# Scores in slot 19 instead of 23 of a two-layer graph kernel's schedule, with the steps that depend on x at other places in the engines' slots

## The reference, cut to what matters

```python
# layer 0
mask = (adj > 0); deg = sum(mask, axis=1)
agg  = mask @ x / max(deg, 1)
out0 = relu(concat(x @ W_self + b_self, agg @ W_nb + b_nb) @ W_comb + b_comb)
x    = layernorm(x + out0)
# layer 1
neib_att = tanh(neigh @ Wn1 + bn1) @ Wn2 + bn2        # 4096 x 32
value    = neigh @ Wv + bv                            # 4096 x 128
x_att    = tanh(x @ Wx1 + bx1) @ Wx2 + bx2
ws       = leaky_relu(x_att @ neib_att.T, 0.01)
ws       = softmax(where(adj > 0, ws, -9e15), axis=1)
out1     = concat(x @ Wfx + bfx, ws @ value)
result   = layernorm(x + out1)
```

## Time and profile before

| | |
|---|---|
| median of 3 runs | 730.26 us (730.22 to 730.64) |
| the profiled execution | 730.62 us, its span 728.8 us |
| PE busy | 689.6 us, 95% of the span |
| DVE busy | 621.7 us, 85% |
| ACT busy | 573.5 us, 79% |
| POOL busy | 129.9 us, 18% |
| chain that ended last | PE 86%, ACT 5%, DVE 4%, issue 3% |
| TensorE clock granted, mean | 0.994 of full |

### The profile page before, as it was taken

How to read it: one execution, slowest core, us unless ns; L and a number is a source line. 1 busy time by engine, 2 the same in 40 slices (tenths; PEclk the granted TensorE clock), 3 DMA queues, 4 the chain that set the end, 5 groups by cost and what they waited for, 6 DMA issues and landing times.

```text
span 728.8 us, 19763 instructions
## 1 busy us (share of the span) xinstructions
PE 689.6 (95%) x7344; PEld 592.1 (81%) x7344; DVE 621.7 (85%) x1535; ACT 573.5 (79%) x920; POOL 129.9 (18%) x242
## 2 busy tenths in 40 slices
PE   5989998999999999999999999999999999998775
PEld 4646676888888888888888888888888888886554
DVE  4887668999999999999999999999999999987874
ACT  2455248888888888888888888888888888889884
POOL 0010111222211222221111222211122221111101
PEclk9989999999999999999999999999999999999999
DMA  8967999999999999999999999999999999841111
GB/s 266 370 150 165 228 269 236 195 203 223 196 202 206 223 208 202 216 224 213 220 212 208 208 203 219 188 221 205 206 200 217 212 220 217 167 81 33 39 42 44
DMA packets 260145, 141.39 MB, mean 194 GB/s; under 512 B 225361, under 2 KB 243665, under 8 KB 260049
## 3 DMA queue, kind: packets, MB, share of 16 engines
q1 hardware_dynamic: 259604, 140.10, 88.7%
q10 hardware_dynamic: 444, 0.02, 0.0%
HBM read 81.35 MB, written 4.19 MB: 117 GB/s over the span
## 4 chain that ended last, share of the span: by engine, by line
PE 86%; ACT 5%; DVE 4%; issue 3%; POOL 1%; DMA 1%; SPq 0%; POOLq 0%; ACTq 0%
PE ps_v L1137 22%; PE ps_agg L1092 15%; PE ps_agg L1095 14%; PE ps_t L1116 10%; PE ps_s L1107 7%; PE ps_agg L1156 3%; PE ps_agg L1159 3%; PE ps_s L1006 2%; PE ps_v L1014 2%; PE ps_x L1176 1%; PE ps_x L1179 1%; ACT score L913 1%; PE ps_t L997 1%; PE ps_x L1023 1%; DMA neigh_sb<-in_L_gnn_neigh_dram 1%
## 5 line engine op out<-in xcount | busy, mean ns | idle before, releaser
L1092 PE MATMUL ps_agg<-x,mask_t 128*128 128x257 f16 x1024 | 243.4, 274 | 0.2 <-DMA mask_t<-mask 0.2
L1095 PE MATMUL ps_agg<-x,mask_t 128*128 128x256 f16 x1024 | 237.4, 273 | 0.3 <-DVE x L533 0.3
L907 ACT ACTIVATE score<-ps_s,sc 128x512 f32<-128x512 f32 x256 | 178.7, 698 | 63.1 <-PE ps_s L1107 57.6
L692 DVE CUSTOM_DVE_ANT_0 score<-score,mask 128x512 f32<-128x512 f32 x256 | 175.9, 687 | 16.7 <-ACT score L907 14.3
L1137 PEld LDWEIGHTS ps_v<-v,late 128*128 128x128 f16 x2304 | 143.9, 97 | 41.7 <-DVE late L756 16.9
L1137 PE MATMUL ps_v<-v,late 128*128 128x129 f16 (+1 forms) x2304 | 162.6, 219 | 11.6 <-DVE late L773 6.0
L913 ACT ACTIVATE score<-score,exp_bias,sc 128x1024 f32<-128x1024 f32 x128 | 159.4, 1246 | 3.2 <-DVE exp_bias L701 3.2
L756 DVE TENSOR_TENSOR late<-ps_t,late 128x512 f16<-128x512 f32 x192 | 130.7, 681 | 33.2 <-ACT late L920 31.4
L920 ACT CAST late<-ps_t 128x512 f16<-128x512 f32 x192 | 114.8, 598 | 20.4 <-PE ps_t L1116 20.4
L1116 PE MATMUL ps_t<-ident,score 128*128 128x128 f32 x768 | 116.8, 275 | 5.3 <-ACT score L913 5.1
L1095 PEld LDWEIGHTS ps_agg<-x,mask_t 128*128 128x128 fp8e4 x1024 | 100.3, 98 | 15.5 <-issue 5.2
(11 more groups left out here) (133 smaller groups left out, 805.4 us busy)
## 6 DMA issues: line engine op xcount, KB each, us to landing
adj_sb<-in_adj_dram SPq DMA_DIRECT2D x128, 512.0 KB, 5.3
neigh_sb<-in_L_gnn_neigh_dram SPq DMA_DIRECT2D x8, 512.0 KB, 8.0
score<-in_x_dram SPq DMA_DIRECT2D x8, 512.0 KB, 8.5
x_in<-in_x_dram SPq DMA_DIRECT2D x32, 128.0 KB, 2.7
out_dram<-out_sb SPq DMA_DIRECT2D x32, 128.0 KB, 3.3
mask_t<-mask SPq DMA_TRANSPOSE x128, 4.8
neigh_sb<-neigh_sb SPq DMA_TRANSPOSE x64, 3.7
mask<-in_L_gnn_W_comb_dram SPq DMA_DIRECT2D x1, 512.0 KB, 9.2
```

The lines of the kernel that those rows point to most:

```text
L692: dve.tensor_tensor_reduce(score[:, b % 2, part], score[:, b % 2, part], mask[:, b % MASK_BUFS, part], 1.0, -3.0e38, ALU.subtract, ALU.max ...
L907: act.activation(score[:, b % 2, k * GW:(k + 1) * GW], ps_s[k % 2][:, :], ACT.Prelu, alpha=SLOPE, scale=score_scale).then_inc(leaky_made, 1)
L1092: mm = pe.matmul(agg[:, 0:D + 1], mask_t8[:, c, 0, :], x16[:, c, X_HI:X_ONE + 1], start=(c == 0), stop=(c == NC - 1), skip_group_check=True)
L1095: mm = pe.matmul(agg[:, 0:D], mask_t8[:, c, 0, :], x16[:, c, X_LO:X_LO + D], start=False, stop=False, skip_group_check=True)
```

## The change

The positions of the steps behind the aggregation are moved closer together, so that the scores start in slot 19. The third and fourth quarter of the masks stand in slots -3 and -1. In PE's slot the steps that depend on x are last. In ACT's slot the exps are first, and mean_of stands ahead of leaky; in DVE's slot row_max is the first of the short steps and degrees, one slot earlier, the last. Names and values after it:

```diff
-MASK_SLOTS = (-7, -5, -1, 0)
+MASK_SLOTS = (-7, -5, -3, -1)
 MEAN_AT = 8
 MEAN_T_AT = 9
 MEAN_SPLIT_AT = 10
-MEAN_LOW_AT = 11
+MEAN_LOW_AT = 10
 X_TURN_AT = 4
-COMBINE_AT = 12
-LAYER0_AT = 13
+COMBINE_AT = 10
+LAYER0_AT = 11
 X1_AT = 15
-X1_T_AT = 16
-X1_COPY_AT = 17
-X1_LOW_AT = 18
-HIDDEN_AT = 19
-TANH_AT = 20
-XATT_AT = 21
-STACK_AT = 22
-SCORE_AT = 23
-ROW_MAX_AT = 31
-TURN_AT = 33
-WEIGH_AT = 34
+X1_T_AT = 15
+X1_COPY_AT = 16
+X1_LOW_AT = 16
+HIDDEN_AT = 16
+TANH_AT = 17
+XATT_AT = 17
+STACK_AT = 18
+SCORE_AT = 19
+ROW_MAX_AT = 27
+TURN_AT = 29
+WEIGH_AT = 30
...
-WIDE_HIGH_AT = (35,)
-WIDE_LOW_AT = (36,)
-WIDE_TURN_AT = (37,)
-WIDE_WEIGH_AT = (40,)
-LAYER1_AT = 42
+WIDE_HIGH_AT = (31,)
+WIDE_LOW_AT = (32,)
+WIDE_TURN_AT = (33,)
+WIDE_WEIGH_AT = (36,)
+LAYER1_AT = 38
...
@@ DVE's slot
-                if d := due(s, MEAN_AT, 0):
-                    degrees(d[0])
+                if d := due(s, ROW_MAX_AT, 0):
+                    row_max(d[0])
...
-                if d := due(s, ROW_MAX_AT, 0):
-                    row_max(d[0])
...
                 if d := turned_by_pe(s, TURN_AT):
                     p_low(*d)
+                if d := due(s, MEAN_AT - 1, 0):
+                    degrees(d[0])
@@ ACT's slot
                 first_part(s)
+                for at, q in EXPS:
+                    if d := due(s, ROW_MAX_AT + 1 + at, 0):
+                        exps(d[0], q)
                 if d := due(s, MEAN_SPLIT_AT, 0):
                     mean_high(d[0])
...
-                for at, q in EXPS:
-                    if d := due(s, ROW_MAX_AT + 1 + at, 0):
-                        exps(d[0], q)
...
+                if d := due(s, MEAN_AT, 0):
+                    mean_of(d[0])
                 if d := due(s, SCORE_AT):
                     leaky(*d)
-                if d := due(s, MEAN_AT, 0):
-                    mean_of(d[0])
@@ PE's slot
                 if d := due(s, 0):
                     aggregate(*d)
+                if d := due(s, SCORE_AT):
+                    scores(*d)
+                if d := turned_by_pe(s, WEIGH_AT):
+                    weigh_values(*d[0:2])
+                for w, at in enumerate(WIDE_WEIGH_AT):
+                    if (d := due(s, at)) and d[1] < 2:
+                        weigh_values(d[0], BY_PE + 2 * w + d[1])
                 if d := due(s, MEAN_T_AT, 0):
                     mean_transpose(d[0])
...
                 if d := due(s, XATT_AT, 0):
                     x_attention(d[0])
-                if d := due(s, SCORE_AT):
-                    scores(*d)
-                if d := turned_by_pe(s, WEIGH_AT):
-                    weigh_values(*d[0:2])
...
```

More of the change, by code:

```diff
@@ L1202, in _ @@
                     x_attention(d[0])
-                if d := due(s, SCORE_AT):
-                    scores(*d)
-                if d := turned_by_pe(s, WEIGH_AT):
-                    weigh_values(*d[0:2])
-                for w, at in enumerate(WIDE_WEIGH_AT):
-                    if (d := due(s, at)) and d[1] < 2:
-                        weigh_values(d[0], BY_PE + 2 * w + d[1])
 _INS = ['x', 'adj', 'L0_gnn_W_self', 'L0_gnn_b_self', 'L0_gnn_W_nb', 'L0_gnn_b_nb', 'L0_gnn_W_comb', 'L0_gnn_b_comb',
```

## The result

The changed kernel takes 739.57 us (739.41 to 739.68, 4 runs) where the kernel before took 730.24 (730.13 to 730.64, 4 runs) on the same chip: ratio 1.0123, 95% interval 1.011 to 1.0135. That is slower by more than the 0.2% that can be told. The profiled execution took 739.41 us with a span of 737.6, which is 8.8 more than before. The forecast was 738.6.

What follows compares the result with a forecast made beforehand. PE bounds the steady blocks (19.50 us each), ACT and waits between engines the end. -8.9 + 4.9 + 1.0 + 0 + 11.3 = +8.3 us on 730.3 gives 738.6 us; range 727 to 745, likeliest case 732 to 745.

Steps and rivals of the forecast that it cites:

- The new wait: In steady blocks PE's hidden_and_fx waits for DVE's x1_low: 0.42 us in each of 27 blocks, +11.3 us.
- ACT's seven pieces: ACT from slot 14's leaky to x1_high: leaky, normalise1, wide_high, p_high, leaky, normalise2, an exp; 4.68 us.
- The work moved ahead of slot 256: Four slots of scores, turns and weighing now stand ahead of slot 256, where PE has no idle time: +4.9 us.
- the fill: Where the pipeline fills: order of PE's work changes, not its amount; -2 to +3 us, taken as 0.
- The shorter end: Between last aggregation and block 31's first scores, four slots (old 256 to 259) fall away: -8.9 us.
- the +1.0: In the end's 11 remaining slots: mean_of and mean_high of block 31 and x1_high of block 30 are added, +1.0 us.
- The masks at cost 0: Third and fourth mask quarters, made and turned at -3 and -1, cost 0; cover is seven slots, 17 us.
- Steps said to have room: Some 0.4 us for layer1's third step; 0.5 each for tanh_low, mean_low and p_low of the fourth turn.
- Rival 3: A second wait joins, likeliest combine behind mean_low or weighing behind p_low: another +8 us, 746.7 us; chance 0.08.
- Rivals 1 and 2: At hidden: no stall, 727.3 us, chance 0.15; or a stall near 0.1 us, 730.3 us, chance 0.07.
- rival 1: No stall at hidden: ACT's seven pieces take 4.26 us or less, or ACT runs ahead; -3.0, 727.3 us, chance 0.15.

Runs made afterwards that it cites:

- E1: Changed kernel with ACT doing x1_high ahead of the slot's exps, rest kept: 725.52 us, ratio 0.9934 to the kernel before.
- E2: Changed kernel with one extra ACT instruction per block (240 columns, read by nobody) behind normalise1 in slot 15: 754.78 us, ratio 1.0328.
- E11: Changed kernel with normalise2 one slot later, as in E5, and SP's store one slot later too: 727.09 us, ratio 0.9953.
- E6: Kernel before with only the new mask slots (-7, -5, -3, -1): 739.47 us, ratio 1.0128.
- E10: Kernel before with only the third quarter's mask moved, from slot -1 to -3: 739.02 us, ratio 1.0117.
- E9: E1 with the old mask slots (-7, -5, -1, 0): 736.22 us, ratio 1.0066.
- E4: Changed kernel with PE's old order in a slot, x's steps ahead of scores and weighing: 775.84 us, ratio 1.0612.
- E8: E1 with everything from normalise1 on one slot earlier, scores at 18: 742.18 us, ratio 1.0165.
- E5: Changed kernel with normalise2 one slot later, at the end of ACT's slot 40: 730.10 us, ratio 0.9997.
- E12: E8 with mean_low ahead of row_max in DVE's slot: 730.30 us, ratio 0.9997.

## Why the prediction was right, and where it was not

**The new wait** was the step that decided, and it came where it was put. Forecast: ready at 5.57, hidden at 5.99 behind the leaky's scores, a stall of 0.42 us. In the trace the scores of slot 14 start at 513.11; PE is ready 5.59 later, hidden starts 6.00 later, a stall of 0.41. ACT's seven pieces take 4.69 us (513.53 to 518.22) where the sum had 4.68. An estimate by the rule of the Trainium skill (ScalarE: Activation LUTs, section What ACT_TABLE_LOAD costs) was 4.81; the measured 4.69 bears out the sum from the rows. E1, E2 and E11 show that this chain is the cause: shortening it removes the stall, lengthening it adds to it. The term was still slightly small. A block lost 0.45 us and not 0.42, since the first matmuls behind the wait cost about 0.04 more; 27 x 0.45 = 12.15 and not 11.3.

**The work moved ahead of slot 256** (+4.9) and the fill (0) came out right as a sum, partly by luck. Slot 256 starts at 676.03 us where it started at 658.95, 17.08 later, and 12.15 + 4.9 is 17.05. But E1, in which no steady block waits, reaches slot 256 only 4.36 us later than the kernel before. Moved work and fill together thus gave 4.4, and 12.7 came with the late x1_high: 12.15 in the 27 blocks, and about 0.6 in the fill, where the hidden of block 2 waits too (at 120.19). The sum had neither, and the two misses of about 0.5 us cancel. The waits in it did change places as said: combine, x1_transpose and hidden each wait once or twice for up to 1.9 us.

**The shorter end** was forecast at -8.9 + 1.0 = -7.9 and measured 24.87 - 33.13 = -8.26, so the +1.0 was +0.6. ACT does have three instructions more in it than in old slots 260 to 270 (40 and 37) and is busy 0.94 us longer, as forecast. It could have been shorter. In it hidden waits for x1_low:

```profile
678.67 0.54 PE L1176 MATMUL ps_x<-x_t,wx 128*96 128x128 f16 x6 [1.13 <-DVE x_t L734]
696.54 0.54 PE L1176 MATMUL ps_x<-x_t,wx 128*96 128x128 f16 x6 [1.35 <-DVE x_t L734]
```

In E1, where x1_high comes first, these are 0.23 to 0.24 us, and the same stretch takes 23.42, that is -9.7 against before. So the term of +1.0 held only with the changed kernel's order; its true lower bound was below nothing, not 0 as I had it. In sum: 17.08 - 8.26 = 8.8, the difference of the spans; the forecast was 8.3, and the medians are 9.3 apart.

**The masks at cost 0** was right as a number for this change, and its reason was wrong. I counted seven slots of cover between a mask and its readers, and looked at nobody else. E6 and E10 show that the new slots cost the kernel before 9 us, through the pieces on DVE that stand beside them. E9 shows that the old slots would have cost some 10 us in the better form of the changed kernel (736.22 against 725.52, from two series, with E9's runs from 731.68 to 737.95), mostly through SP's queue ahead of the wide turns. The third quarter's mask in slot -3 shares DVE's slot 13, modulo eight 5, with whatever stands there; before it was layer0, and the change moves layer0 to 11. The two edits belong together, and a reader who tries them one by one would reject both.

**Steps said to have room** had it in the changed kernel: no wait of layer1, tanh_low or p_low stops PE in the steady part. Rival 3 did not happen. It is the one that E4 (0.1 us a block) and E8 (0.43) bring about, both through mean_low.

**Rivals 1 and 2** needed the chain to be 0.3 us shorter. In E5 it is 0.49 shorter by one piece, and the stall is gone, as rival 1 said. E11, without the stall and without E5's waits for the turns, ends at 727.09, and rival 1 had 727.3. What rival 1 did not have is that E1's version ends at 725.5; its span is 5.3 below that of before: 9.7 less in the end, 4.36 more until slot 256.

Left open: why the wide turns take longer to land in E9 and in E5, and where the executions of E4 that were not profiled lose their further 1 to 4.7 us.

## What to carry to other kernels

When steps of a software pipeline are brought closer together, count each engine's pieces in order between a producer and the reader, at their start-to-start times from the trace; a gap of 0.4 us that comes back in each block outweighs the whole gain at the end. Put the short piece on which another engine waits ahead of the long ones in its slot: here one place in ACT's order turned +1.2% into -0.7%. And cost a moved piece not by its own readers alone, but by what it lands beside in its engine's slot, and by what stands behind it in the queue that it feeds.

## What the runs showed of the hardware

- A matmul group that had to wait costs PE a little beyond the wait: hidden's first half took 0.37 us from start to start behind the wait and 0.33 without one.
- DVE's masked_scores and POOL's addition meet, and it is the later one that takes longer. In E6 POOL starts first, at 508.48 (0.73 us), and masked_scores at 508.75 takes 1.01 in place of 0.68. In the kernel before, it is the other way round; DVE's row, then POOL's:

```profile
306.55 0.68 DVE L692 CUSTOM_DVE_ANT_0 score<-score,mask 128x512 f32<-128x512 f32 x1
```

```profile
306.93 0.89 POOL L468 TENSOR_TENSOR late<-x,bfv_sb 128x256 f32<-128x256 f32 x1 [1.51 <-ACT x L931]
```

  Here DVE keeps its 0.68 and POOL takes 0.89. In the changed kernel the two do not meet, and POOL takes 0.72. The Trainium skill (SBUF — State Buffer, section Who interferes with whom) says that a DVE instruction with two inputs in SBUF contends with a POOL instruction that reads SBUF, and that the order of issue decides which of the two is blocked. The rows agree on who loses. A full block, which the page states for DVE's two-port modes, would have held masked_scores until POOL's end at 509.21, 0.46 us, and it lost 0.33.
- In the fill of E8 PE waited 2.43 us before x1_transpose, which starts at 88.14, and from 89 to 91 us its granted clock was 0.50 of full, the lower of its two levels (1.2 GHz). E12 waited the same 2.43 us at the same place and kept 1.00 from 85 to 92 us, and E1 waited 1.89 and kept 1.00. So the length of that wait alone does not tell whether the clock falls; what does was not found.
- The wide turns landed 5.6 us after their issue (median) in E9 and 4.0 in E1. In both, a mask turn, a load and a store stand ahead of them in the queue, with the mask turn issued 2.8 us ahead in E9 and 3.4 in E1. Whether that makes the difference was not tried.
